# GNN stack of four layers: first edges sought by lanes, edge rows cleared and placed in two parts, one TensorE loop written out

## What is computed

```
edge_index = jnp.stack([src, dst])          # dst sorted ascending
x = _layernorm(x + _L0_gnn_ref(x, src, dst, edge_weight, ...))
x = _layernorm(x + _L1_gnn_ref(x, edge_index, edge_type_4, ...))
x = _layernorm(x + _L2_gnn_ref(x, edge_index, ...))
x = _layernorm(x + _L3_gnn_ref(x, edge_weight, src, dst, ...))
# layer 0, its edge part
msgs = edge_val[:, None] * x[edge_col]
agg = jax.ops.segment_sum(msgs, edge_row, num_segments=N)    # edge_col = dst, edge_row = src
# layer 3, its edge part
msgs = z[edge_dst] @ Wd + z[edge_src] @ Ws + edge_weight[:, None] * ww[None, :] + bm
agg = jax.ops.segment_max(msgs, edge_dst, num_segments=n)
```

## Time and profile before

| | us |
|---|---|
| three runs, median | 4789.67 |
| lowest, highest | 4785.03, 4798.37 |
| the profiled execution, whole | 4801.15 |
| its span, first to last instruction | 4799.3 |
| granted TensorE clock, mean | 0.736 of full speed |

### The profile page before, as it was taken

One profiled execution on the slowest core, in us unless ns is written; L12 is line 12 of the kernel. 1 busy time (PEld: TensorE's weight loads), 2 busy tenths in 40 slices (PEclk: granted clock), 3 DMA queues, 4 the chain that ended last, 5 costly groups with the idle time before them and its releaser, 6 DMA issues. The chain is left out here.

```text
span 4799.3 us, 60694 instructions
## 1 busy us (share of the span) xinstructions
PE 2121.5 (44%) x11977; PEld 1206.2 (25%) x11977; DVE 3583.7 (75%) x7007; ACT 2745.0 (57%) x6085; POOL 3313.6 (69%) x2937
## 2 busy tenths in 40 slices
PE   4499999999853000000000400000000458889995
PEld 3255554444422000000000200000000235555553
DVE  9365665555547899999997588888988657777776
ACT  0388888788722888888884322232222245655663
POOL 0488888888726777777772477777777337777774
PEclk9799999999976555555555755555555679999998
DMA  9655555555633577777674456666666323333332
GB/s 401 207 101 101 105 107 95 97 100 101 129 70 131 212 261 269 270 258 277 255 275 192 141 186 218 217 211 210 217 219 210 97 70 118 118 115 117 126 120 85
DMA packets 281953, 816.71 MB, mean 170 GB/s; under 512 B 62437, under 2 KB 177653, under 8 KB 269554
## 3 DMA queue, kind: packets, MB, share of 16 engines
q1 hardware_dynamic: 102828, 561.89, 31.0%
q0 software_dynamic: 169776, 248.56, 23.7%
q10 hardware_dynamic: 9238, 5.24, 0.5%
HBM read 366.96 MB, written 448.51 MB: 170 GB/s over the span
## 5 line engine op out<-in xcount | busy, mean ns | idle before, releaser
L643 POOL DMA_INDIRECT tab<-arena x560 | 952.4, 1701 | 210.3 <-issue 132.2
L1576 PE MATMUL psum<-ident,arena 128*128 128x128 f32 x15 | 3.7, 428 | 2145.9 <-DVEq L1604 2145.9
L773 PE MATMUL psum<-arena 128*128 128x512 bf16 (+1 forms) x4704 | 949.7, 357 | 0.0
L1948 POOL DMA_INDIRECT arena<-table,arena x784 | 748.1, 954 | 242.4 <-issue 238.5
L2448 POOL DMA_INDIRECT arena<-table,arena x622 | 630.1, 1013 | 191.3 <-issue 179.8
L1331 POOL DMA_INDIRECT arena<-table,arena x588 | 610.2, 1038 | 179.3 <-issue 172.3
L2530 PE MATMUL psum<-arena 128*128 (+1 forms) x4050 | 685.5, 332 | 90.6 <-DVE arena L2578 49.6
L773 PEld LDWEIGHTS psum<-arena 128*128 128x128 bf16 x4704 | 433.7, 99 | 473.6 <-issue 24.6
L1576 PEld LDWEIGHTS psum<-ident,arena 128*128 128x128 f32 x15 | 2.7, 214 | 2146.4 <-DVEq L1604 2146.2
L2530 PEld LDWEIGHTS psum<-arena 128*128 (+1 forms) x4050 | 402.0, 99 | 366.6 <-issue 115.8
L1379 ACT ACTIVATE arena<-arena 128x128 f32<-128x128 f32 x1344 | 408.8, 387 | 92.1 <-DVE arena L1498 88.5
(11 more groups left out here) (426 smaller groups left out, 5164.9 us busy)
## 6 DMA issues: line engine op xcount, KB each, us to landing
rows<-arena SPq DMA_DIRECT2D x56, 3808.0 KB
arena<-seg_rows SPq DMA_DIRECT2D x112, 896.0 KB, 7.1
rows<-arena SPq DMA_DIRECT2D x56, 1008.0 KB, 4.7
seg_rows<-arena SPq DMA_DIRECT2D x28, 1792.0 KB
rows<-arena SPq DMA_DIRECT2D x56, 896.0 KB, 3.9
arena<-table,arena POOLq DMA_INDIRECT x1994
arena<-src_lanes SPq DMA_DIRECT2D x56, 448.0 KB
tab<-arena POOLq DMA_INDIRECT x560
```

Of the source, the lines that this page charges most:

```text
L643: eng.indirect_dma_start(out=m.tabs[j], out_offset=bass.IndirectOffsetOnAxis(ap=idx[g][:, k:k + 1], axis=0), in_=rows[g][:, k, 0:D], in_of ...
L773: t = eng.matmul(ps[:, c, 0:w], part[n // 2 % PAIRS][:, n % 2, :], hot[n % HOTS][:, lo:lo + w], start=False, stop=False, skip_group_check= ...
L1948: eng.indirect_dma_start(out=kv[k][:, j, :], out_offset=None, in_=m.table2, in_offset=bass.IndirectOffsetOnAxis(ap=idx[k][:, j:j + 1], axi ...
```

## The change

In the setup, the counting of degrees goes. Instead:

- PE spreads the first dst of each lane over all partitions (one matmul). DVE compares these 128 with each node number and counts (128 x 25 x 128, one compare, one reduction): the lane in which the node's first edge lies (lane_i).
- dst, centred and as f16, is stored to DRAM as dst_rows [128, 784]. POOL gathers, for each of the 25 blocks, each node's lane row (25 indirect DMAs, rows of 1568 bytes). For each block DVE compares 784 numbers with the node's and counts (within). Lane times 784 plus within is the first edge (start_f).
- The end of a node is the start of the next: two matmuls with shift matrices.
- Of seg_rows only the first 10 of 28 parts (ZEROED) are cleared in the setup. The other 36 half parts (896 KB each) are cleared by SP in turns 0 to 3 of layer 0 (CLEARING), three after each of the four loads of turn 0 and two after each of turns 1 to 3.
- early_start sends to the edge rows only those nodes whose first edge lies in the first 6 turns (EARLY) of its lane, or which have none of their own place; late_start sends the others. The early ones are scattered in the setup, the late ones by POOL in layer 0 between turn 3 and turn 4. Both are 25 DMAs of 128 rows; rows that are not meant go to the spare rows. SP waits for the late ones (late_put) before the loads of turn 5.
- The wait for the clearing moves in SP behind the clearing of the tables, which now waits for S_COUNTED.
- PE's matmuls for the ends stand behind the turning of weights and x.

In layer 3 PE's 25 blocks are written out; block b waits for b + 7 one-hots of the turn (LEAD), at most 25.

The diff, cut:

```
@@ setup, POOL
+                eng.wait_ge(dst_stored, 16)
+                eng.wait_ge(prep, S_LANE)
+                for b in range(NB):
+                    eng.indirect_dma_start(out=lane_rows[:, b, :], out_offset=None, in_=m.dst_rows[:, :],
+                                           in_offset=bass.IndirectOffsetOnAxis(ap=lane_i[:, b:b + 1], axis=0)).then_inc(rows_in[b // BY], 16)
...
-                                           out_offset=bass.IndirectOffsetOnAxis(ap=m.start[:, b:b + 1], axis=0),
+                                           out_offset=bass.IndirectOffsetOnAxis(ap=early_start[:, b:b + 1], axis=0),
@@ setup, SP
-                eng.wait_ge(const, 1)
-                with eng.Fori(0, TURNS) as i:
+                eng.wait_ge(prep, S_DSTC)
+                eng.dma_start(m.dst_rows[:, :], dst_c).then_inc(dst_stored, 16)
+                eng.wait_ge(const, 17)
+                with eng.Fori(0, ZEROED) as i:
...
-                eng.wait_ge(zeroed, 16 * ZEROS)
+                eng.wait_ge(prep, S_COUNTED)
@@ setup, DVE
-                with eng.Fori(0, TURNS) as i:
-                    for h in range(2):
...
+                step(eng.tensor_tensor(under, spread(ps[:, 7, 0:P], 1, [P, NB, P]), spread(node_f, 2, [P, NB, P]), ALU.is_lt))
+                step(eng.tensor_reduce(lane_n, under, AX.X, ALU.add))
...
+                for b in range(NB):
+                    if b % BY == 0:
+                        eng.wait_ge(rows_in[b // BY], 16 * BY)
+                    step(eng.tensor_scalar(lane_rows[:, b, :], lane_rows[:, b, :], node_c[:, b:b + 1], None, ALU.is_lt))
+                    last = step(eng.tensor_reduce(within[:, b:b + 1], lane_rows[:, b, :], AX.X, ALU.add))
@@ layer 0, SP
+                def clear_some(point):
+                    for c in left[point::4 * CLEARING]:
+                        eng.dma_start(lanes(m.seg_rows)[:, c * HALF:(c + 1) * HALF, :].rearrange("p t f -> p (t f)"),
+                                      zeros[:, 0:HALF * D]).then_inc(rows_cleared, 16)
...
+                eng.wait_ge(late_put, 16 * NB)
@@ layer 0, POOL
-                with eng.Fori(0, TURNS) as i:
+                with eng.Fori(0, CLEARING) as i:
+                    turn(i)
+
+                eng.wait_ge(rows_cleared, 16 * 2 * (TURNS - ZEROED))
+                for b in range(NB):
+                    eng.indirect_dma_start(out=m.seg_rows, out_offset=bass.IndirectOffsetOnAxis(ap=m.late_start[:, b:b + 1], axis=0),
+                                           in_=m.xN[:, b, :], in_offset=None).then_inc(late_put, 16)
+                with eng.Fori(CLEARING, TURNS) as i:
+                    turn(i)
@@ layer 3, PE
-                    with eng.Fori(0, (NB - 1) // TOGETHER - 1) as g:
-                        hold(eng, hot_made, i * NB - NB + g * TOGETHER + TOGETHER + 1)
-                        for n in range(TOGETHER):
-                            block_sums(g, 1 + n)
+                    for b in range(NB):
+                        eng.wait_ge(hot_made, i * NB - NB + min(b + LEAD, NB))
+                        for p, part in enumerate(parts):
```

More of the change, by code:

```diff
@@ L213, in setup_phase @@
         prev_lastf = A(1)
-        iota = A(P, dt=BF16)
-        iota_i = A(P, dt=I32)
-        nul = A(P, dt=BF16)
+        dst_c = A(T, dt=F16)
+        node_f, node_c = A(NB), A(NB)
+        lane_rows = A(NB, T, dt=F16)
+        under = A(NB, P)
+        lane_n, lane_f, within = A(NB), A(NB), A(NB)
+        lane_i = A(NB, dt=I32)
+        start_f = A(NB + 1)
+        over, early = A(NB), A(NB)
+        next_lane, corner = A(P), A(P)
+        early_start = A(NB, dt=I32)
         spare_start = A(NB)
@@ L494, in _ @@
                 step(eng.tensor_copy(m.lane_first[:, :], dst[:, 0:1]))
+                for b in range(NB):
[3 more added lines that the diff above has]
+                    last = step(eng.tensor_reduce(within[:, b:b + 1], lane_rows[:, b, :], AX.X, ALU.add))
+                assert last == S_COUNTED
+                assert step(eng.scalar_tensor_tensor(out=start_f[:, 0:NB], in0=lane_f, scalar=float(T), in1=within, op0=ALU.mult, op1=ALU.add)) == S_STARTF
+                eng.wait_ge(ends_done, 1)
+                step(eng.tensor_copy(end1, ps[:, 6, 0:NB]))
+                step(eng.tensor_tensor(deg, end1, start_f[:, 0:NB], ALU.subtract))
+                step(eng.tensor_scalar(m.has[:, :], deg, 1.0, None, ALU.min))
+                step(eng.tensor_tensor(tmp, start_f[:, 0:NB], spare_start, ALU.subtract))
+                step(eng.tensor_tensor(tmp, tmp, m.has[:, :], ALU.mult))
+                step(eng.tensor_tensor(m.start[:, :], tmp, spare_start, ALU.add))
+                step(eng.tensor_scalar(early, within, float(EARLY * BODY), None, ALU.is_lt))
+                step(eng.tensor_scalar(over, within, float(T), None, ALU.is_equal))
+                step(eng.tensor_tensor(early, early, over, ALU.add))
+                step(eng.tensor_tensor(over, tmp, early, ALU.mult))
+                assert step(eng.tensor_tensor(early_start, over, spare_start, ALU.add)) == S_START
+                step(eng.tensor_tensor(tmp, tmp, over, ALU.subtract))
+                step(eng.tensor_tensor(m.late_start[:, :], tmp, spare_start, ALU.add))
+                step(eng.scalar_tensor_tensor(out=tmp, in0=end1, scalar=float(-1 - EP), in1=m.has[:, :], op0=ALU.add, op1=ALU.mult))
+                step(eng.tensor_scalar(m.end[:, :], tmp, float(EP), None, ALU.add))
                 eng.wait_ge(l_edge, 16 * 6)
@@ L509 @@
 SRCB = 112
-LOW, HIGH = 64, 2 * NB
-S_HALVES = 7
-S_DEG = 8
-S_START = 17
-S_WHOLE = 21
-assert 2 * LOW == P and HIGH <= P
-ZEROS = TURNS + 6
+BY = 5
+S_DSTF, S_DSTC, S_LANE, S_WHOLE = 1, 2, 5, 9
+S_COUNTED = 21 + 2 * NB
+S_STARTF = S_COUNTED + 1
+S_START = S_STARTF + 11
+assert NB % BY == 0
+ZEROED, CLEARING, EARLY = 10, 4, 6
+ZEROS = ZEROED + 6
+assert CLEARING < EARLY <= ZEROED
 SMALL = len(COLUMNS) + 1 + len(ROWS) + 1 + 5 + 1
@@ L632, in _, with turn @@
                     eng.dma_start(m.tabs[j][NP:NP + P, :], zeros[:, 0:D]).then_inc(added[j], 16)
-                with eng.Fori(0, TURNS) as i:
+                def turn(i):
                     for g in range(GROUPS):
@@ L2378, in layer3_edges @@
         tab = A(NB, D)
-        part_cols = [A(NB * D, dt=BF16) for _ in range(3)]
-        parts = [part.rearrange("p (b f) -> p b f", f=D) for part in part_cols]
+        parts = [A(NB, D, dt=BF16) for _ in range(3)]
         keys = A(BATCH, dt=F16)
-        hot_cols = A(NB * BATCH, dt=BF16)
-        hot = [hot_cols[:, b * BATCH:(b + 1) * BATCH] for b in range(NB)]
+        hot = [A(BATCH, dt=BF16) for _ in range(NB)]
         turned_rows = A(BATCH)
@@ L2525, in _ @@
             def _(eng):
-                def block_sums(g, n, first=False, last=False):
-                    for p, part in enumerate(part_cols):
-                        for c, w in CHOPS:
-                            t = eng.matmul(found[:, c:c + w], part[:, bass.ds(g * (TOGETHER * D) + n * D, D)],
-                                           hot_cols[:, bass.ds(g * (TOGETHER * BATCH) + n * BATCH + c, w)],
-                                           start=(first and p == 0), stop=(last and n == TOGETHER and p == 2))
-                    t.then_inc(hot_used, 1)
                 eng.nop().then_inc(turned, 1)
@@ L2538, in _ @@
                 with eng.Fori(1, TURNS) as i:
[L2539 to L2547 removed]
+                    for b in range(NB):
+                        eng.wait_ge(hot_made, i * NB - NB + min(b + LEAD, NB))
+                        for p, part in enumerate(parts):
+                            for c, w in CHOPS:
+                                t = eng.matmul(found[:, c:c + w], part[:, b, :], hot[b][:, c:c + w], start=(b == 0 and p == 0),
+                                               stop=(b == NB - 1 and p == 2))
+                        t.then_inc(hot_used, 1)
                     eng.wait_ge(evicted, i)
```

156 lines of the change are left out of this document (59 added, 97 removed).

## The result

| | before | after |
|---|---|---|
| 16 runs each, median, us | 4792.96 | 4808.44 |
| lowest, highest | 4780.48, 4808.00 | 4796.66, 4826.86 |
| span of the profiled execution | 4799.3 | 4809.9 |

A forecast was written before the change was run, and what follows sets the result against it. Setup was taken as bound by clearing seg_rows, layer 0 and layer 3's edges by POOL. Setup -52, late scatters +32, clearing +25 and layer 3 0 sum to +5: 4795 us from a median of 4789.67, range 4770 to 4833.

The forecast's parts named there:

- no change as the likeliest case: Whole kernel: time the same as before, within about 0.3% (14 us); chance 0.45.
- the case given 0.35: Whole kernel: slower than before by more than about 0.3% (14 us); chance 0.35.
- Setup, -52: Setup: the new chain starts the first scatter at 92 instead of 145.83; -52 us, bounds -60 and -37.
- Late scatters, +32: Layer 0: 25 more indirect DMAs in POOL's text, paid in full; +32 us, bounds 31 and 36.
- The port rival: Setup and layer 0: wide DVE steps and one-hots hold POOL, 8 and 11 us; sum +22, 4812; chance 0.07.
- Clearing, +25: Layer 0: 36 clearing DMAs delay the landing of POOL's adds; +25 us.
- the middle of the three bounds: Layer 0's clearing: each of 36 clearings costs one add 0.65 us, 23 us, between low 14 and high 49.
- PE's long text: Layer 3: written-out blocks make PE's turn 30 us, longer than POOL's 29; +27, 4822; chance 0.03.
- Layer 3, 0: Layer 3: PE finishes a microsecond or two later or earlier, DVE's sums wait for gathers anyway; 0 us.
- The bounds of ±8 for held gathers: Layer 3: a shifted DVE phase adds or removes three gathers of 3.61 us, 2.7 us each; -8 to +8.
- 20 us below 4789.67: Whole kernel: clearing nearly free (14 us), setup -58, sum -12, with layer 3 kindly -20, 4772; chance 0.20.
- the long-stretch rival: Layer 0: clearing costs 45 instead of 25, or setup gathers 9 us more; sum +30, 4820; chance 0.25.

The follow-up runs named there:

- layer3_only: The kernel before with only layer 3's PE text written out, lead of 7 one-hots: 4799.39 us, ratio 1.0006.
- split_loop: The kernel after with all 28 parts cleared in the setup, without late scatters and SP's wait for them; single execution, layer 0's edges 1152.8 us.
- lead1: The kernel after with LEAD = 1 instead of 7, so block b waits for one more one-hot: 4797.68 us, ratio 1.0019.
- idx_first: The kernel after with ACT making the next half 0 indices ahead of taking out PE's sums in layer 3: 4785.53 us, ratio 0.9988.
- prep_only: The kernel after with before's layer 3, so only the new setup and layer 0: 4801.07 us, ratio 1.0012.
- idx_first_before_b: The kernel before with ACT making the next half 0 indices ahead of taking out PE's sums, on the third chip: 4779.41 us, ratio 0.9984.
- clear_ahead: The kernel after with all 28 parts of seg_rows cleared in the setup, late scatters kept; single execution on the second chip, layer 0's edges 1196.4 us.

## Why the prediction was right, and which term was off

The forecast was 4795 with no change as the likeliest case (0.45). The time came out at 4808.4, inside the range, and on the slow side of the 0.3% by a hair, the case given 0.35. Of the 13.4 us between the two, 3.3 are the base: the median of before is 4792.96 over 16 runs, where three gave 4789.67.

- **Setup, -52: right to 0.1 us**, and by its own steps: the first gather at 19, groups of lane rows, counting to 88, both chains meeting there, the first scatter at 92, 41.2 us from there to the first load (39.6 before). The packet-by-packet sharing of three queues, from which the landing of the gathers was worked out, is in the trace. That the sum is right to 0.1 us is luck in part: the third group of gathers was there 1.6 us earlier than put (64.4 for 66) and the fourth 4.4 later (73.4 for 69), for which DVE waited 1.7, and the two cancel; the weights came 1.6 us behind the latest time given and were done only just before the count.
- **Late scatters, +32: right** (33.0, and 32.6 by the starts). The trace shows no stall ahead or behind. The port rival had them caught by one-hots for 11 us: 25.4 us of busy time for 25 leave no room for it. In the setup, where that rival put 8 us and the forecast 2, the first four scatters were held for 3.2 us above 0.97 each.
- **Clearing, +25: right** (26.4; 28 to 32 against the kernels that clear ahead), and the middle of the three bounds was the right row to go by. Its mechanism, a fixed loss for each of 36 DMAs, was not: 44 cost no more. So the figure was right in part by luck. Adds did not come at 2.6 us or more either, but at 2.43 on average (191.7 / 79; before 2.09).
- **PE's long text** as the bound: not seen on any chip that runs layer 3 at its usual pace. The 100 matmuls of the last timeline row took 16.75 us, 24.5 us for 147 with the 47 ahead of them, the pace of rows 11.
- **Layer 3, 0: the step that failed.** The prediction said that PE ends a microsecond or two earlier or later and "DVE's sums wait for gathers anyway". That looked at DVE alone. The consumer that mattered was ACT, which makes POOL's next indices behind PE's sums; rows 11 of before name it (ACT arena L2475, 7.6 us), and as waits of 0.3 us these were read as part of the fixed gap rather than as an engine that comes just in time. The cost is in the idle time of the gathers: 198.7, 202.9 and 201.8 us in the three traces with LEAD = 7 and indices last on the usual chips (after, layer3_only, split_loop), 190.1 to 194.6 in the seven others. That is about 8 us, and lead1 and idx_first take it away by two different edits. The waits for ACT above the fixed 0.30 us say the same more sharply: 5.5, 10.1 and 7.9 us in the three, at most 0.9 in the seven.
- **The bounds of ±8 for held gathers** were too narrow. The busy time of the same 622 gathers was 609.7 to 631.2 us over ten traces, a spread of 21.5 us. The runs of one kernel spread by 28 to 30 us from lowest to highest in the table at the top; these held gathers and the 17 us in layer 0's later turns are large enough for that, though one profile for each kernel can't prove it.
- **Slips in the rivals' sums**, which moved nothing: 20 us below 4789.67 is 4770 and not 4772, and the long-stretch rival names 45 us but adds 42.

So the sum of the profiled pair is -52.0 + 55.0 + 1.3 + 8.4 - 2.1 = +10.6, where the forecast had +5. The medians lie 15.5 apart, 5 us more. An estimate from the stages alone comes near that: -52.0 for the setup, +26.5 for the clearing, +32.6 for the late scatters and +7.4 of idle time in layer 3 are +14.5; the profiled pair is lower by the 4 us in layer 0's later turns, where executions differ by up to 17. The times of the parts don't prove it: prep_only and layer3_only alone cost 1.0012 and 1.0006, which together make 1.0018 and not 1.0033; with intervals of about 0.0013 around each, that is no contradiction and no proof of an interaction.

On chips of the usual pace no variant beat the kernel before by more than can be measured. The nearest are idx_first_before_b (0.9984, up to 1.0000) and idx_first (0.9988, up to 1.0001).

## What to carry to other kernels

Work moved out of a serial setup is not free in a phase that another engine bounds. What goes into that engine's own text is paid there in full (33 us for the second set of scatters), and what only runs beside it can still hold it up (26 us for the transfers). Against 52 us won, the exchange was a loss by its own sum, before layer 3 came into it. Where an engine's row numbers or addresses for the bottleneck are made behind its waiting for a third engine, make them first, even if the profile shows only waits of 0.3 us: such a wait costs nothing, but it tells that the engine has no slack there. Here that was worth nothing that could be measured on the usual chips, and 3.4% on the one whose PE is late. And when a term of a sum is smaller than the spread of held instructions in one execution, read busy and idle time of the group apart, since one trace can hide the one behind the other.

## What the runs showed of the hardware

- Three DMA queues that all have work move one packet each in turn (515, 516 and 517 packets in 20 us), though a packet of the clearing is about 13 KB and one of the gathers about 3. The Trainium skill ("DMA: Bandwidth & Descriptors", Queues, rings and completion order) states this for an engine's queues; the trace agrees for three.
- Adds lose no more with the DMA engines at 377 GB/s than at 239 GB/s. That fits a price for a queue in use rather than for its bytes; no run here takes the two apart.
- How many of 622 gathers are held ranges from 2 to 12 on the usual chips, for texts whose POOL parts are the same. It was the largest difference between executions that I found in layer 3. At most one in a trace takes 5.5 us, beside DVE's wide f32 steps at the start of layer 3. The other 54 of the ten traces take 2.7 to 3.6 us and have one pattern: each starts 0.18 to 1.2 us after DVE began a run of eleven one-hots (50 of them within 0.4 us) and ends 0.12 us behind the whole run's end, not behind one instruction's. Yet running at once is not enough: in before, 246 gathers overlap a one-hot and 9 are held, and of gathers that start 0.2 us into a run some are held and some take 1.02 us. What decides is open. On the second chip none was held so.
- On the second chip PE's written-out matmuls of layer 3 stand apart by 2.5 us for stretches, without a wait, while other stretches run as elsewhere. From the timeline of clear_ahead:

```profile
4919.75 0.58 PE L2558 MATMUL psum<-arena 128*128 128x512 bf16 x1 [2.59 <-issue]
...
4922.60 0.37 PE L2558 MATMUL psum<-arena 128*128 128x256 bf16 x1 [2.26 <-issue]
```

The kernel before, whose PE text is a loop there, is 22% slower on that chip as well, so the written-out text is not the cause. What is, no run here shows.
